# Router logits with the router's columns held still and the tokens streamed, and the slot table built from the selection in expert order

## The reference

```python
mu = x.mean(-1, keepdims=True)
var = x.var(-1, keepdims=True)
h = (x - mu) * jax.lax.rsqrt(var + 1e-05) * ln_g + ln_b
m_t = h.mean(1, keepdims=True)          # over the 512 tokens of a batch
v_t = h.var(1, keepdims=True)
h_norm = (h - m_t) * jax.lax.rsqrt(v_t + 1e-08)
...
h = h_norm * gamma[:, None, :] + beta[:, None, :]   # gamma, beta: a small net of the subject
probs = jax.nn.softmax(h_flat @ router_w, axis=-1)  # 8 experts
gates, idx = jax.lax.top_k(probs, 2)
gates = gates / gates.sum(-1, keepdims=True)
hid = jax.nn.relu(jnp.einsum('nd,edf->nef', h_flat, exp_w1) + exp_b1)   # 256 -> 1024
eout = jnp.einsum('nef,efd->ned', hid, exp_w2) + exp_b2                 # 1024 -> 256
y = jnp.einsum('ned,ne->nd', eout, combine)
return x + y.reshape(x.shape)
```

## Time and profile before

| | us |
|---|---|
| median of 3 runs | 516.13 (515.57 to 517.37) |
| profiled execution | 517.13 |
| its span, first to last instruction | 515.3 |
| mean granted TensorE clock | 0.935 of 2.4 GHz |

### The profile page before, as it was taken

One profiled execution on the slowest core, in us unless ns is written; L12 is line 12 of the kernel. 1 busy time (PEld: TensorE's weight loads), 2 busy tenths in 40 slices (PEclk: granted clock), 3 DMA queues, 4 the chain that ended last, 5 costly groups with the idle time before them and its releaser, 6 DMA issues.

```text
span 515.3 us, 16220 instructions
## 1 busy us (share of the span) xinstructions
PE 479.5 (93%) x5818; PEld 444.2 (86%) x5818; DVE 394.2 (76%) x1431; ACT 277.3 (54%) x836; POOL 258.6 (50%) x331
## 2 busy tenths in 40 slices
PE   7888996799989999999999999999999999999990
PEld 4688983699978999999999999899999989999990
DVE  4876348889887888888888888888888887777550
ACT  2554432566654656665666566556665655454540
POOL 0632113156654655565556565656565655455532
PEclk8776567999998999999999999999999999999996
DMA  8941246544443434444444444344434332323221
GB/s 314 391 165 42 82 146 149 162 91 104 95 87 77 99 85 94 92 109 87 92 105 94 87 93 108 92 87 91 110 89 92 68 54 44 51 46 54 33 32 21
DMA packets 37822, 51.71 MB, mean 100 GB/s; under 512 B 8064, under 2 KB 29840, under 8 KB 37488
## 3 DMA queue, kind: packets, MB, share of 16 engines
q0 software_dynamic: 13632, 18.91, 21.8%
q1 hardware_dynamic: 22016, 31.17, 19.0%
q10 hardware_dynamic: 2096, 0.60, 0.4%
HBM read 36.74 MB, written 18.11 MB: 106 GB/s over the span
## 4 chain that ended last, share of the span: by engine, by line
PE 87%; DVE 5%; DMA 3%; issue 1%; ACT 1%; POOL 1%; DVEq 0%; SPq 0%; ACTq 0%; POOLq 0%
PE bank L696 37%; PE bank L703 36%; PE bank L529 3%; PE bank L651 3%; PE bank L540 2%; PE bank L511 2%; PE bank L645 2%; PE bank L520 1%; DMA par<-in_params 1%; DMA out_rows<-yout,tok 1%; DVE tns L794 1%; DMA hg<-h_rows,tok 1%; DVE wlo L1033 0%; DVE hidlo L1048 0%; POOL whi L291 0%
## 5 line engine op out<-in xcount | busy, mean ns | idle before, releaser
L466 ACT ACTIVATE hid<-bank,par 128x128 f32<-128x128 f32 x568 | 162.5, 369 | 169.5 <-PE bank L696 169.3
L696 PE MATMUL bank<-hThi,whi 128*128 128x128 f16 x1136 | 188.3, 219 | 5.2 <-DVE wlo L1033 1.7
L696 PE MATMUL bank<-hTlo,whi 128*128 128x128 f16 x1136 | 188.2, 219 | 0.0
L696 PE MATMUL bank<-hThi,wlo 128*128 128x128 f16 x1136 | 156.4, 219 | 0.0
L703 PE MATMUL bank<-whi,hidlo 128*128 (+1 forms) x568 | 155.1, 273 | 0.0
L703 PE MATMUL bank<-whi,hidhi 128*128 (+1 forms) x568 | 155.1, 273 | 0.0
L703 PE MATMUL bank<-wlo,hidhi 128*128 (+1 forms) x568 | 155.1, 273 | 0.0
L342 POOL DMA_INDIRECT out_rows<-yout,tok x71 | 115.6, 1628 | 34.0 <-issue 33.2
L326 POOL TENSOR_TENSOR held_gp<-zero 1x1 f32<-1x1 f32 x142 | 50.5, 356 | 148.0 <-DVE tok L1024 94.1
L696 PEld LDWEIGHTS bank<-hThi,whi 128*128 (+1 forms) x1136 | 111.0, 98 | 15.3 <-issue 7.9
L1043 DVE CAST hidhi<-hid 128x512 f16<-128x512 f32 x142 | 71.4, 503 | 60.1 <-ACT hid L466 59.9
(11 more groups left out here) (163 smaller groups left out, 536.1 us busy)
## 6 DMA issues: line engine op xcount, KB each, us to landing
stage<-in_exp_w SPq DMA_DIRECT2D x64, 256.0 KB
whi<-in_x SPq DMA_DIRECT2D x8, 512.0 KB, 8.8
out_rows<-in_x SPq DMA_DIRECT2D x8, 512.0 KB, 16.3
h_rows<-wlo SPq DMA_DIRECT2D x8, 512.0 KB, 3.8
hg<-h_rows,tok POOLq DMA_INDIRECT x71, 3.3
out_rows<-yout,tok POOLq DMA_INDIRECT x71
b2row<-in_exp_b SPq DMA_DIRECT2D x1, 1024.0 KB, 20.7
par<-in_params SPq DMA_DIRECT2D x1, 493.5 KB, 6.5
```

The costliest lines, as they stand in the source:

```text
L466: ins = S(hid32[:, par, c * P:(c + 1) * P], bk_hid[half][:, (c - 4 * half) * P:(c - 4 * half + 1) * P], ACT.Relu, bias=vcol[:, bass.ds(e * ...
L696: hid_ins = MM(o, lhs[w, k], h[:, par, k * P:(k + 1) * P], start=(n == 0), stop=(n == 3 * KD - 1))
```

## The change

There are four parts.

1. The logits change roles. The router's matrix, padded from 8 to 32 columns (`EP`), is the stationary operand, and 512 tokens are streamed: 2 products for a batch in place of 8. Batch `i` of a part writes the 32 PSUM partitions from `32 i`, by `tile_position`. Four batches make a part (`BP` = 4), so that a part fills 128 partitions. ACT copies them (`copy_logits`), and PE turns them into token-major form by 4 transposes for a part (`logits_of_tokens`). All `warm` products between the logits are gone (18), and of the 20 behind the count 10 are left.
2. The slot table keeps `selh` in expert order. Starts of the experts come from 8x8 comparisons of the counts on DVE; the prefix matrices of PE work within an expert's 32 columns and need no padded counts. The loads of expert numbers into DVE's registers shrink to one number and move behind the second lookup. `reciprocal(1)` comes later in DVE's order.
3. The function `ahead` is gone: tile `t + 3` is looked up in every tile `t`, `NHG` is 4. In tiles 0 and 1 DVE splits weights before it looks up a tile, and PE makes that slot table behind the tile's products.
4. `rank_starts` moves from tile 0 to tile 2 and begins with two more small instructions.

The first place is PE's order from the logits of batch 4 to the end of the front, before and after (L529 and L533 are logits, L540 and L550 are `back`, L511 `warm`; in the new program L540 is `logits_of_tokens` and L524 is `transposes`).

The diff, cut to its core:

```diff
-BP = 5
+BP = 4
+EP = 32
-NHG = 5
-LEAD4 = 10
+NHG = 4
...
+            def copy_logits(part):
+                act.wait_ge(s_lgt, BP * (part + 1))
+                S(lgT[part], bk_log[part][:, 0:T], ACT.Copy).then_inc(s_lgs, 1)
...
-            def logits(b, half):
-                if half == 0:
-                    pe.wait_ge(s_h2, 2 * b + 2)
-                for j in range(2 * half, 2 * half + 2):
-                    for k in range(KD):
-                        at = (b * JB + j) * E
-                        ins = MM(bk_log[b // BP][:, at:at + E], hT[b][:, k * T + j * P:k * T + (j + 1) * P], rw[:, k * E:(k + 1) * E],
-                                 start=(k == 0), stop=(k == KD - 1))
+            def logits(b):
+                pe.wait_ge(s_h2, 2 * b + 2 if b < BP else max(2 * b + 2, 12))
+                i = b % BP
+                for k in range(KD):
+                    ins = MM(bk_log[b // BP][EP * i:EP * i + EP, 0:T], rw[:, k * EP:(k + 1) * EP], hT[b][:, k * T:(k + 1) * T],
+                             start=(k == 0), stop=(k == KD - 1), tile_position=(0, EP * i))
+                ins.then_inc(s_lgt, 1)
+
+            def logits_of_tokens(part):
+                pe.wait_ge(s_lgs, part + 1)
+                for j in range(JB):
+                    ins = nc.tensor.transpose(bk_log[part][:, j * P:(j + 1) * P], lgT[part][:, j * P:(j + 1) * P], ident)
                 ins.then_inc(s_log, 1)
...
-            for k in range(E):
-                ins = V.tensor_copy(selp[:, 1 + k * NJ:1 + (k + 1) * NJ], selh[:, bass.ds(order[k] * NJ, NJ)])
-            ins.then_inc(s_perm, 1)
...
+            n_above = mark(V.tensor_tensor(above, by_column(key), by_row(key), ALU.is_gt))
+            n_rank = mark(V.tensor_reduce(rank, above, AX_X, ALU.add))
+            n_starts = mark(V.tensor_tensor(starts, above, by_column(nei[:, 5, :]), ALU.mult))
+            n_start = mark(V.tensor_reduce(start, starts, AX_X, ALU.add))
...
             slot_steps(2, 0)
             at = lookup(1, at)
             slot_steps(3, 1)
+            first = expert_numbers(ve, nei[0:1, 2, 0:1])
             w_lo(0)
             w_lo(1)
...
-                for u in ahead(t)[0:1]:
-                    slot_table(u, u % 2)
+                if 2 <= t < TILES - 3:
+                    slot_table(t + 3, (t + 3) % 2)
                 products(1, tile(t), e0, tile(t - 1), e1)
-                for u in ahead(t)[1:2]:
-                    slot_table(u, u % 2)
+                if t < 2:
+                    slot_table(t + 3, (t + 3) % 2)
```

More of the change, by code:

```diff
@@ L354, in _ @@
                     scatter(t - 2)
-                for u in ahead(t):
-                    gather(u)
+                if t + 3 < TILES:
+                    gather(t + 3)
             gp.wait_ge(s_sc, 16 * TILES)
@@ L437, in _ @@
             modulate(4)
+            copy_logits(0)
             modulate(5)
@@ L446, in _ @@
             router_exp(0, *PARTS[0])
+            copy_logits(1)
             for b in range(4, 6):
@@ L989, in _ @@
-            V.tensor_tensor(ca16[:, :], bk_col[:, 0:NH], adj[:, 0, :], ALU.add).then_inc(s_ca, 1)
-            ve.wait_ge(s_col, 1)
-            link(V.tensor_copy(stcol[:, :], bk_col[:, 4:8]))
-            ve.wait_ge(s_dp, 1)
+            sel3 = selh[:, :].rearrange("p (e j) -> p e j", e=E)
+            dsel3 = dsel[:, :].rearrange("p (e j) -> p e j", e=E)
+            ve.wait_ge(s_sel, 2)
+            V.tensor_tensor(dsel3[:, :, 1:NJ], sel3[:, :, 1:NJ], sel3[:, :, 0:NJ - 1], ALU.subtract)
+            cnt, key, keys, less, padcnt, rank, start, gap = (es8[:, i, :] for i in range(8))
@@ new lines, in _, with by_row, by_column @@
+            above, starts, prev, last_of, gap_of = (ee[:, i, :, :] for i in range(5))
+            def by_row(a):
+                return a.unsqueeze(2).broadcast_to([P, E, E])
+            def by_column(a):
+                return a.unsqueeze(1).broadcast_to([P, E, E])
+            ve.wait_ge(s_cnt, 1)
+            cnt3 = bk_cnt[:, 0:NBLK].rearrange("p (e j) -> p e j", e=E)
+            link(V.tensor_reduce(cnt, cnt3, AX_X, ALU.add))
+            n = mark(V.scalar_tensor_tensor(out=key, in0=cnt, scalar=float(E), in1=cst[:, C_KEY:C_KEY + E], op0=ALU.mult, op1=ALU.add))
@@ new lines, in _ @@
+            ve.wait_ge(s_v, n_less)
+            n_pc = mark(V.scalar_tensor_tensor(out=padcnt, in0=nei[:, 5, :], scalar=1.0 / E, in1=less, op0=ALU.mult, op1=ALU.add))
+            ve.wait_ge(s_v, n_start)
+            for h in range(NH):
+                ins = V.tensor_tensor_reduce(ne[:, 6 + h, :], start, cst[:, C_OF + h * E:C_OF + (h + 1) * E], 1.0, 0.0,
+                                             ALU.mult, ALU.add, scol[:, h:h + 1])
+            n_of = mark(ins)
+            ve.wait_ge(s_v, n_last)
@@ L1105, in _ @@
             ve.wait_ge(s_b2, 16)
-            es = [order[0]] * 6
+            es = [first[0]] * 6
             for t in range(TILES):
@@ L1112, in _ @@
                     es = expert_numbers(ve, etile[0:1, t:t + 6])
-                par, other, to = t % 2, 1 - t % 2, ahead(t)
-                tokens = len(to) > 0
+                par, other = t % 2, 1 - t % 2
+                tokens = 2 <= t < TILES - 3
                 gate(t, es[2 + t % 4])
@@ L1119, in _ @@
                 if tokens:
-                    tokens_compare(to[0])
+                    tokens_compare(t + 3)
                 if t + 1 < TILES:
                     tile_lo(t + 1, other)
-                if t >= 1 and tokens and to[0] + 1 < TILES:
-                    slot_steps(to[0] + 1, (to[0] + 1) % 2)
+                if t < 2:
+                    for i in chunks_of(t):
+                        w_lo(i)
+                elif t + 4 < TILES:
+                    slot_steps(t + 4, par)
                 split_lo(par, 0, at + 1)
@@ L1143, in _ @@
                         w_lo(i)
-                for u in to[1:2]:
-                    at = lookup(u, at)
-                    slot_steps(u + 1, (u + 1) % 2)
-                if t == 0:
+                else:
+                    at = lookup(t + 3, at)
+                    if t == 1:
+                        slot_steps(5, 1)
+                if t == 2:
                     rank_starts()
@@ L1175, in constants @@
     for i, v in enumerate((pair % NJ // JB, pair % JB)):
[L1176 removed]
+        step = np.diff(v, prepend=v[-1])
         for h in range(NH):
@@ L1183, in constants @@
     c[:, C_KEY:C_KEY + E] = E - 1 - np.arange(E)
-    for k in range(E):
-        at = k * NJ + NJ - 1
-        c[at % P, C_LAST + at // P * E + k] = 1 / E
+    for h in range(NH):
+        of = (h * P + q) // NJ
+        c[q, C_OF + h * E + of] = 1 / E
+        first = q % NJ == 0
+        c[q[first], C_FIRST + h * E + of[first]] = 1
     c[:, C_EPS], c[:, C_EPS + 1] = LN_EPS, T_EPS
-    c16 = np.zeros((P, 5 * P), np.float16)
+    c16 = np.zeros((P, 4 * P), np.float16)
     c16[:, 0:P] = q[:, None] <= q
     c16[:, P:2 * P] = 1
-    c16[:, 2 * P:3 * P] = q[:, None] < q
-    c16[:, 3 * P:4 * P] = q[:, None] == q - 1
-    c16[P - 1, 4 * P] = 1
+    same = q[:, None] // NJ == q // NJ
+    c16[:, 2 * P:3 * P] = same & (q[:, None] < q)
+    c16[:, 3 * P:4 * P] = same & (q[:, None] == q - 1)
     return c, c16
```

171 lines of the change are left out of this document (90 added, 81 removed).

## The result

| | before | after |
|---|---|---|
| median, runs of both on one chip | 516.75 us (515.57 to 517.63, 4 runs) | 495.09 us (494.95 to 496.67, 4 runs) |
| span of the profiled execution | 515.3 | 493.1 |
| mean granted clock | 0.935 | 0.977 |

The ratio is 0.9589, 95% interval 0.956 to 0.9619. The forecast was 495.5.

A forecast was written before the change was run, and what follows sets the result against it. PE was taken to hold 87% of the chain, the front at clock 0.60; -15.3 + 0.3 - 1.5 - 4.2 = -20.7 us took the profiled 517.13 to 496.4, given as a 495.5 us median, range 489 to 515.

The forecast's parts named there:

- The clock: Front: streamed logits no cheaper at equal clock, but keep PE at 2.4 GHz from 28 to about 52 us.
- The walk: Front stepped through by engine at 2.4 GHz, bringing the count to DVE at 59.2 us in place of 74.56.
- Low clock: Rival, front: streams fill 32 of 128 columns and the clock stays at 1.2 GHz; 514.7 us, chance 0.14.
- Clock up and down: Rival, front: faster PE waits for ACT and POOL, half the front's gain goes; 505 us, chance 0.13.
- dear stream: Rivals, front logits: twice the transposes' price; high clock 507 us, chance 0.05; low clock 539 us, chance 0.09.
- The front's size: Term for the front up to the count's arrival on DVE: -15.3 us.
- The second hop: Front, part 1's logits: copy_logits(1) and four transposes, new on the path, about 1.3 us.
- The slot table: Term from the count to tile 0: shorter table chain, its gain lost again; +0.3 us (-1.0 to +1.5).
- two covers end at the same time: Ahead of tile 0: DVE's register load, w_lo(0), tile_lo(0), and the gates with first gather 10.3 us after the count.
- Tiles 0 to 2: Term: -2.0 us in tiles 0 and 1, +0.5 in tile 2 for rank_starts; -1.5 us (-2.5 to +0.5).
- Tile 10: Term: the double lookup that holds PE up in tile 10 is gone; -4.2 us (-3.5 to -4.5).
- The mode change: Front: possible array drain at 16 tiling changes, a tenth of a us each; 1.6 us more, 497.1.

The follow-up runs named there:

- e3: The changed kernel with narrow logits (8 streamed columns) again, without the copy, the logits' transposes or products of zeros: 506.44 us.
- e4: The changed kernel with every logits product given twice, the second pair overwriting the first with the same values: 506.95 us.
- e1: The kernel before with the lookup always three tiles ahead, five gather buffers kept: 512.74 us against 516.84.
- e8: The changed kernel with reciprocal(1) ahead of the chain of comparisons on DVE, as in the kernel before: 494.66 us.
- e9: The kernel before with streamed logits and a lead of three tiles; slot table, order in tiles 0 and 1 and rank_starts as before: 496.7 us.
- e2: The kernel before with the streamed logits alone; slot table, lead and tiles as before: 501.24 us.
- e10: The changed kernel with rank_starts back in tile 0 instead of tile 2: 496.96 us.
- e7: The changed kernel with 29 f32 transposes of the identity added behind the 6 products of zeros ahead of tile 0: 495.07 us.
- e11: The changed kernel with the reciprocal early and two of the four last gate stores issued by POOL instead of ACT: 495.88 us.

## Why the prediction was right, and where it was not

**The clock: right.** The forecast was that the narrow form and the stream cost PE the same at one clock, and that the stream keeps the high one. 1.83 us stand against 1.8; the front is at 1.00; e3 takes the streams away and has 0.50 to 0.74 and 11 us more; e4 doubles them and still has 1.00. The walk did not say what the order and the 18 products of zeros are worth without the stream; by e3 and e1 that is 6.3 us of the time. "Low clock", "Clock up and down" and both cases of a "dear stream" are out.

**The front's size: too small.** -15.3 was charged. The two profiles show -18.3 (74.56 to 56.29), of which up to 1.6 us is when the count comes in executions of one kernel: e1's front, unchanged, was at 73.12, and the changed kernel's three at 56.29, 56.80 and 57.87. The means of these are 73.84 and 56.99, -16.9 us. The walk failed at its end. It let the logits' own transposes end at 53.2; they ended at 51.2, of which 1.4 us is the earlier start. And it let the seven `back` groups reach 58.8, behind the selection's 58.1; in the trace `selh` ends last and the count's product follows 0.14 us behind it.

The second hop was charged 1.3 us and took that, copy (L419, done at 50.54) and transposes (50.58, 0.67 us). It comes right behind the load of ACT's table (48.44, 1.28 us), not behind the last logits: those of batches 6 and 7 ran side by side and ended at 49.34, where the walk has them one after the other.

**The slot table: right in sum, its path partly.** +0.3 was charged, "two covers end at the same time". Tile 0's first product is 14.59 us behind the count (56.29 to 70.88), before it was 14.57 (74.56 to 89.13). The first gather was to come 10.3 us behind it and came 9.9. The terms of the 10.3 were off and made up for each other: the reciprocal came 2.8 us behind the count (59.07), charged 4.2, and the last of the gate stores landed 3.44 us behind its issue (61.74 to 65.18), charged 2.7. The chain to the first table product was charged 6.0 us and took 4.8 (61.10); it is not on the path. The gates are one of the two covers, and e8 shows it by taking one us from them. The other was named wrong. DVE's register load, then `w_lo(0)` and `tile_lo(0)`, were to be as late; in the trace `w_lo(0)` waits for ACT's half of the weights, and `hTlo` (70.40) follows ACT's `hThi` (69.98), which follows the gather.

**Tiles 0 to 2: wrong.** -1.5 was charged (-2.0 in tiles 0 and 1, +0.5 in tile 2). From the first gather to tile 12's the kernel before took 65.46 us, the new one 66.17, +0.7. The failed step is the -2.0 of tiles 0 and 1. Up to tile 5's gather the gain was 0.1 us (25.69 to 25.58). The step counted DVE's work from tile 0's start as if PE entered tile 0 as before. But PE idles 3.8 us before it and does the first 24 products at 1.2 GHz. PE's wait for `w_lo(7)` was to end 9.9 us behind tile 0's first product, where it was 11.9; it ends 11.1 behind it (70.88 to 81.99).

Four executions take the step apart, each against the one before it. The old order at the high clock takes 25.72 us (e9), at the low clock 26.88 (e2): +1.2 for the clock. The new order, with `rank_starts` still in tile 0 and the low clock, takes 27.10 (e10): +0.2. With `rank_starts` moved it is 25.58 to 25.76: -1.3 to -1.5. So the new order of lookups and splits won nothing; the gain read from DVE's program was the move of `rank_starts`, and the clock took most of it back. In the new order the clock is worth less, 0.7 us by e7. e2, e9, e10 and e7 have one profile each.

The +0.5 of tile 2 was nearly right. There DVE's row of small instructions stands in the chain (timeline of DVE, first and last):

```profile
91.48 0.18 DVE L1104 TENSOR_SCALAR nei<-es 128x8 int32<-128x8 f32 x1
...
92.66 0.16 DVE L1111 TENSOR_TENSOR ne<-ne 128x7 f32<-128x7 f32 x1
```

That is 1.3 us of DVE, and from tile 5's gather on 0.8 us of the time (39.77 to 40.59), which e10 gets back.

**Tile 10: right.** -4.2 was charged. The gather given out in tile 9 (tile 12's) moved by 17.8 us, from 150.17 to 132.38; the one given out in tile 11 by 22.0, from 165.67 to 143.65. The difference is 4.2. e1 has 4.1 by itself. The shorter lead costs nothing here: after tile 0 the changed kernel has no wait for `hg` up to 140 us in any of its three profiles.

**The sum.** By one pair of profiles, with the slot table read up to the first gather: -18.3 - 0.2 + 0.7 - 4.2 = -22.0, and the spans differ by 22.2. By the comparisons of the runs, 21.7, 21.4 and 20.3 us. The forecast's -20.7 came from a front 1.6 us too small and tiles 2 us too good.

**The mode change.** The sum with a tenth of a us at each change would have been 1.6 us more. There are 14 changes and not 16, as nothing stands between batches 6 and 7. e4 gives a bound: four more records in the same mode add 1.72 us (3.55 in place of 1.83), so going in and out adds at most 0.11 us a batch, 0.8 us of PE's time over the front. Whether that is a drain cannot be told, because the ends of products are modelled in the profile.

**The rivals' sums.** Two do not come out of their terms. The low clock's 3.2 + 1.7 + 1.3 - 3.9 is 2.3 us, not 4, so its time is 513.0. "Clock up and down", half of the front's 15.3 given back, is 503.2, not 505. Neither touches the forecast.

## What to carry to other kernels

Price a form of product twice: at one clock, and by whether it keeps the clock. Here two forms with the same cost at 2.4 GHz (1.69 and 1.83 us a batch) were 11 us apart over eight batches, because the one whose time is weight loads did not keep that clock. And take out what only fills time before crediting the new form: a third (by the medians) to a half (by the profiles) of the front's gain came without the stream. Where two chains end at the same wait, a faster one buys nothing: see which is last now, which is next, and which is behind that, as the third here stood 0.15 us behind the second. And an idle stretch ahead of dense products can have a second price, the products at half speed behind it; look whether the next engine's pace hides it before filling it. Look at the clock before comparing two profiles, too: e2 and e9, one program in tile 0, differ there by 1.2 us.

## What the runs showed that was not expected

- Transposes on PE hold the clock: 29 of them in 67.15 to 70.48 us, and 1.00 up to 75 us (e7), where the kernel without them fell to 0.50 ahead of tile 0. In the kernel before it rose from 0.50 to 1.00 at the end of 3.4 us of nothing else.
- Products that write different groups of 32 partitions run side by side: batches 6 and 7 took 2.05 us together, one batch alone 1.83.
- A product with 32 stationary columns and 512 streamed f32 columns keeps the clock at 1.00 for 40 us (28 to 68 us in e4), although it fills a quarter of the array's columns.
- The last gate store of 16 KB in a row lands later than the median one: 3.44 us after its issue in the changed kernel (61.74 above), whose four on ACT have a median of 2.7 us, as the earlier trace rows. With two of them moved to a third queue (e11) the medians of the three queues were 3.6 to 4.0 us, and the first gather came only 0.15 us earlier.
- The same instructions of the front start up to 1.6 us apart in executions of one kernel, already at the first transposes (22.58, 22.62 and 24.11 us for the third batch's, in three executions of the changed kernel). The clock's first rise is where they part: it came just before 17.0 us in the first of these and at 19.5 in the third, whose first eight transposes took 1.92 us in place of 1.18. The kernel before had it at 18.3 us, e1 just before 17.0, and their counts are 1.4 us apart.
